# Second cross attention: turning the probabilities against a diagonal of inverse sums

## The chip, the cores and the metric

The kernel runs on one core of one Trainium2 chip. The metric is the device time of one launch in microseconds (us), and less is better. A core has five engines that run their own instruction streams and wait for each other by semaphores: TensorE (PE in the profile, with PEld for its weight loads), VectorE (DVE), ScalarE (ACT), GpSimd (POOL) and SyncE (SP). Each stream is executed in the order in which it was written, so an instruction that waits holds up all behind it on its engine.

## The reference, cut to what matters

Two decoder layers of width 128 over 4 batches of 512 tokens, with a context of 77 rows. The part around the change is the cross attention of the second layer: 8 heads of 64, 512 queries that come from the tokens, and 512 + 77 keys.

```python
xn = layernorm(x, gm, bm)                      # x here: the context, 77 rows
ln = layernorm(latents, gl, bl)                # latents: the 512 tokens
q = ln @ Wq
kv_input = jnp.concatenate([xn, ln], axis=-2)  # 589 keys
k, v = jnp.split(kv_input @ Wkv, 2, axis=-1)
q, k, v = (heads(q), heads(k), heads(v))
sim = jnp.einsum('bhid,bhjd->bhij', q / scale, k)
sim = sim - jnp.max(sim, axis=-1, keepdims=True)
attn = jax.nn.softmax(sim, axis=-1)
out = jnp.einsum('bhij,bhjd->bhid', attn, v)
return out @ Wout                              # heads joined again
```

## The kernel before

All data of a batch stay in SBUF, and each engine's program is written out by hand; batches follow each other in a loop of four. Every matrix product here is in fp32. The second cross attention works on 32 units per batch (`UNITS`). Unit i is one head and one tile of 128 queries; two units of a loop turn j, 2j and 2j + 1, are the two heads of a pair v = j // 4 for query tile t = j % 4. Three PSUM regions and three probability buffers `PBX` are used in turn by i % 3.

A unit goes round the engines like this:

- PE, `scores(j)` (L1355 and L1361): scores of both units against 512 token keys and 77 context keys. It waits until exp(2j - 2) has left its PSUM region and `move_context(2j - 2)` is done.
- DVE, `maximum(i)` (L2223): the negated row maximum over 589 columns.
- ACT, `exp(i)` (L1777): exponentials into `PBX`, with the row's sum added up into column i of `xsums` (the trace shows a second instruction that reads the accumulator).
- PE, `turn(k)` (L1367 and L1371): the context part (77 columns) and the four 128x128 blocks are transposed against the identity, into PSUM.
- ACT, `move_context(k)` (L1785) and DVE, `move(k)` (L2230): the turned parts go to SBUF, to `PTC` and `PTX`. `turn(k)` waits until `move(k - 1)` has emptied bank 6.
- PE, `value(v, c)` (L1386): values of pair v with chunk c of the turned probabilities, added up over the five chunks in bank 7; each pair's chunks are spread over the turns of the next pair.
- ACT, `copy_values(v)` (L1789): the values of pairs 0 to 2 go to `OT`.

PE's order in turn j is scores(j), turn(2j - 1), a projection of values in the first five turns, up to two value chunks, turn(2j). DVE's is maximum(2j), move(2j - 1), maximum(2j + 1), move(2j). ACT's is move_context(2j - 1), exp(2j), move_context(2j), exp(2j + 1), and then copies.

The probabilities are turned before they are divided by their sums; the division comes at the end, on the values. The inverse sums are made in two pieces (`invert_sums`, L2214). `spread_inverse(v)` (L1400) brings them to the layout of the values: 8 products of a broadcast column with the identity for each pair. DVE multiplies pairs 0 to 2 (`normalise`, L2219). The factors of the last pair are copied to `last_factors` by ACT (L1804) and multiplied in by DVE (L2247). PE then runs value(3, 0 to 4), `project_pairs(0, 3)` and `project_pairs(3, 1)` (L1407), and DVE adds the result to the residual (L2249).

Other lines that appear in the rows: L1494 is a product of the expert network with 128x128 operands; L1719 and L1723 are ACT copies from PSUM in other stages, the second with a bias of one value per partition; L1608 is an ACT operation on a 128x128 tile within SBUF.

Of the kernel before, what the change touches and what calls it, by code (L numbers as in the profile page):

```python
# [9 lines left out]
ALU = mybir.AluOpType  # L10
ACT = mybir.ActivationFunctionType
# [24 lines left out]
def decoder_kernel(nc, x, ctx_1024, qkv_w, qkv_b, qn_scale, qn_bias, kn_scale, kn_bias, ttt_gate, ttt_val,  # L36
# [4 lines left out]
    with stack:  # L41
# [3 lines left out]
        def sem(name):  # L45
            return stack.enter_context(nc.semaphore(name))
# [214 lines left out]
        def first_turn(n):  # L261
# [10 lines left out]
                             "probs_T_ready", "values_ready", "values_copied"))  # L272

        UNITS, XG = 4 * 8, 8
        s_xi, s_xsp, s_xn, s_xfac, s_cturned = (
            sem("x1_" + n) for n in ("sums_inverted", "spread", "values_normalised", "factors_moved", "context_turned"))

        (m_parts, m_picked, m_stacked, m_scores, m_max, m_split, m_turned, m_rows, m_scoresT, m_exp, m_acc01,
         m_acc, m_sums, m_inv, m_spread, m_norm, m_values, m_outs) = (sem("m_" + w) for w in (
# [409 lines left out]
        PTX = [PTA[:, 2048 * r:2048 * r + 2048].rearrange("p (k q) -> p k q", k=4) for r in range(3)]  # L689
        PTX.append(OTA[:, 2048:4096].rearrange("p (k q) -> p k q", k=4))  # L690
        PTC = KMA[:, 2560:4608].rearrange("p (h q) -> p h q", h=4)
        last_factors = QXA[:, 0:512]
        PT0 = [buf[0:CTX, at:at + 2048].rearrange("p (g q) -> p g q", g=4)
               for buf, at in ((PTA, 4096), (VA, 0), (VA, 2048), (OTA, 2048))]
        Y0 = KMA[:, 0:512].rearrange("p (t d) -> p t d", d=D)
# [255 lines left out]
        def _(pe):  # L951
# [320 lines left out]
            for b in range(BATCH):  # L1272
# [90 lines left out]
                    last.then_inc(s_scores, 1)  # L1363

                def turn(k):
                    pe.wait_ge(s_exp, b * UNITS + k + 1)
                    T.transpose(PSUM[0:CTX, 2 * (k % 3) + 1, P:2 * P], PBX[k % 3][:, SEQ:XK], ident[:, :]).then_inc(s_cturned, 1)  # L1367
                    if k:
                        pe.wait_ge(s_moved, b * UNITS + k)
                    for c in range(4):  # L1370
                        last = T.transpose(PSUM[:, 6, c * P:(c + 1) * P], PBX[k % 3][:, c * P:(c + 1) * P], ident[:, :])  # L1371
                    last.then_inc(s_turned, 1)

                def value(v, c):
                    if c == 0:
                        pe.wait_ge(s_moved, b * UNITS + XG * (v + 1))
                        pe.wait_ge(s_cmoved, b * UNITS + XG * (v + 1))
                        if v:
                            pe.wait_ge(s_outs, b * 3 + v)
                        else:  # L1380
                            pe.wait_ge(s_e_vs, b * 5 + 5)
                    rows = P if c < 4 else CTX
                    for e in range(2):
                        h = 2 * v + e
                        probs = PTX[h % 4][:, c, :] if c < 4 else PTC[0:CTX, h % 4, :]
                        last = T.matmul(PSUM[e * XD:(e + 1) * XD, 7, :], VX[0:rows, c, h * XD:(h + 1) * XD],  # L1386
                                        probs, start=(c == 0), stop=(c == 4))
                    if c == 4:
                        last.then_inc(s_values, 1)

                def spread_inverse(v):
                    k = (4, 5, 2, 0)[v]
                    pe.wait_ge(s_cmoved, b * UNITS + UNITS - 2)
                    if v >= 2:
                        pe.wait_ge(s_exp, b * UNITS + UNITS)
                    pe.wait_ge(s_xi, b * 2 + (2 if v == 3 else 1))
                    for t in range(QT):
                        for e in range(2):
                            i = XG * v + 2 * t + e
                            last = T.matmul(PSUM[e * XD:(e + 1) * XD, k, t * P:(t + 1) * P],  # L1400
                                            xsums[:, i:i + 1].to_broadcast([P, XD]), ident[:, :], start=True, stop=True)
                    last.then_inc(s_xsp, 1)

                def project_pairs(first, n):
                    for v in range(first, first + n):
# [5 lines left out]
                for j in range(UNITS // 2 + 1):  # L1411
# [9 lines left out]
                            value(pair, c)  # L1421
                    if j < UNITS // 2:
                        turn(2 * j)
                for v in range(4):
                    spread_inverse(v)
                for c in range(5):
                    value(3, c)
                pe.wait_ge(s_xfac, b + 1)
                pe.wait_ge(s_xn, b * 4 + 3)
                project_pairs(0, 3)  # L1430
                pe.wait_ge(s_xn, b * 4 + 4)
                project_pairs(3, 1)


# [139 lines left out]
        def _(act):  # L1574
# [169 lines left out]
            for b in range(BATCH):  # L1744
# [35 lines left out]
                def move_context(k):  # L1780
                    (v, t), e = divmod(k // 2, QT), k % 2
                    act.wait_ge(s_cturned, b * UNITS + k + 1)
                    if v >= 2 and t == 0 and e == 0:
                        act.wait_ge(s_values, b * 4 + v - 1)
                    A.activation(PTC[0:CTX, (2 * v + e) % 4, t * P:(t + 1) * P], PSUM[0:CTX, 2 * (k % 3) + 1, P:2 * P], ACT.Copy)                        .then_inc(s_cmoved, 1)  # L1785

                def copy_values(v):
                    act.wait_ge(s_values, b * 4 + v + 1)
                    A.activation(OT[:, v, :], bank(7), ACT.Copy).then_inc(s_outs, 1)  # L1789

                for j in range(UNITS // 2):
                    if j:
                        move_context(2 * j - 1)
                    exp(2 * j)
                    move_context(2 * j)
                    exp(2 * j + 1)
                    if j < 5:
                        copy_projected(j)
                    if j >= 8 and j % QT == 0:
                        copy_values(j // QT - 2)  # L1800
                move_context(UNITS - 1)
                copy_values(2)
                act.wait_ge(s_xsp, b * 4 + 4)
                A.activation(last_factors, bank(0), ACT.Copy).then_inc(s_xfac, 1)  # L1804


                rows_T()
# [60 lines left out]
        def _(dve):  # L1868
# [301 lines left out]
            for b in range(BATCH):  # L2170
# [36 lines left out]
                for p in range(4):  # L2207
                    dve.wait_ge(s_e_k, b * 4 + p + 1)
                    kb = 512 * (4 + 2 * (p % 2))
                    Vv.tensor_copy(KX[:, p, :], PSF[:, kb:kb + XK]).then_inc(s_e_ks, 1)  # L2210
                def invert_sums(first, n):
                    dve.wait_ge(s_exp, b * UNITS + XG * (first + n))
                    sums = xsums[:, XG * first:XG * (first + n)]
                    Vv.reciprocal(sums, sums).then_inc(s_xi, 1)  # L2214

                def normalise(v):
                    dve.wait_ge(s_xsp, b * 4 + v + 1)
                    dve.wait_ge(s_outs, b * 3 + v + 1)
                    Vv.tensor_tensor(OT[:, v, :], OT[:, v, :], bank((4, 5, 2)[v]), ALU.mult).then_inc(s_xn, 1)  # L2219

                def maximum(i):
                    at = 1024 * (i % 3)
# [9 lines left out]
                for j in range(UNITS // 2):  # L2232
                    dve.wait_ge(s_scores, b * (UNITS // 2) + j + 1)
                    maximum(2 * j)
                    if j:
                        move(2 * j - 1)
                    maximum(2 * j + 1)
                    if j == UNITS // 2 - 2:
                        invert_sums(0, 3)
                    move(2 * j)  # L2240
                move(UNITS - 1)
                invert_sums(3, 1)
                for v in range(3):
                    normalise(v)
                dve.wait_ge(s_xfac, b + 1)
                dve.wait_ge(s_values, b * 4 + 4)
                Vv.tensor_tensor(OT[:, 3, :], bank(7), last_factors, ALU.mult).then_inc(s_xn, 1)  # L2247
                dve.wait_ge(s_e_o, b + 1)
                Vv.tensor_tensor(xs, PSUM[:, 0:4, 0:D], xs, ALU.add)  # L2249

# [142 lines left out]
```

## Time and profile before

| what | us |
|---|---|
| median of 3 runs | 2002.82 |
| lowest and highest run | 2001.36, 2003.3 |
| the profiled execution, its own time | 2002.89 |
| its span in the trace | 2001.2 |
| TensorE, busy | 1747.9 (87%) |
| VectorE, busy | 1084.5 (54%) |
| ScalarE, busy | 845.2 (42%) |
| GpSimd, busy | 514.9 (26%) |
| mean granted TensorE clock | 0.935 of full |

The times above are of whole launches; the span runs from the first to the last instruction in the trace. Busy times are sums over stages of different kinds. The changed stage occurs four times, once per batch; the first one begins at 654.32 us of the span and its last instruction, the add of L2249, starts at 730.82.

### The profile page before, as it was taken

The page shows a single profiled execution, that of the slowest core. Times are in us where ns is not written, and L with a number is a line of the kernel's source. Part 1 is how long each engine was busy: PE and PEld are TensorE (multiplying, and loading weights), DVE is VectorE, ACT ScalarE, POOL GpSimd, SP SyncE. Part 2 cuts the span into 40 slices and gives each one's busy share as a digit, 9 for nine tenths or more (in the row PEclk, how much of TensorE's full clock was granted, in tenths as well). Part 3 has the DMA queues.
Part 4 walks back from the last instruction along what each step waited for, and adds up shares of the span by engine and source line. Part 5 has one row for each costly group of instructions (what it writes and reads, how often), then busy time and mean ns, then how long its engine had stood idle before and what let it go on. Part 6 is the DMA issues. An engine that isn't in the chain of part 4 may idle for free.

```text
span 2001.2 us, 27188 instructions
## 1 busy us (share of the span) xinstructions
PE 1747.9 (87%) x10505; PEld 996.0 (50%) x10505; DVE 1084.5 (54%) x2162; ACT 845.2 (42%) x1406; POOL 514.9 (26%) x574
## 2 busy tenths in 40 slices
PE   4599789896898988898989889998988998989888
PEld 3354645553434555573455546634555473455556
DVE  4577467464463656346646553563646346646542
ACT  2222222222463536345635444463536345635442
POOL 2377077230063003003700120063003002700120
PEclk7799899897889999898999899989999898999999
DMA  7000000000000000000000000000000000000000
GB/s 212 0 1 1 1 0 0 0 1 1 0 1 1 1 1 2 1 1 6 1 1 1 1 1 1 6 1 1 1 1 1 1 1 6 1 1 1 1 1 6
DMA packets 18260, 13.27 MB, mean 7 GB/s; under 512 B 7643, under 2 KB 14783, under 8 KB 18143
## 3 DMA queue, kind: packets, MB, share of 16 engines
q1 hardware_dynamic: 17951, 11.65, 2.1%
q8 instruction: 79, 1.29, 0.3%
q14 instruction: 38, 0.31, 0.1%
q10 hardware_dynamic: 192, 0.02, 0.0%
HBM read 10.55 MB, written 1.05 MB: 6 GB/s over the span
## 4 chain that ended last, share of the span: by engine, by line
PE 65%; issue 10%; DVE 7%; POOL 6%; ACT 6%; POOLq 5%; DVEq 1%; DMA 0%; SPq 0%
PE PSUM L1307 7%; PE PSUM L1484 6%; PE PSUM L1494 5%; PE PSUM L429 4%; PE PSUM L1386 4%; PE PSUM L1355 3%; PE PSUM L385 3%; PE PSUM L1371 2%; POOLq L873 2%; POOLq L871 2%; POOL OTA L875 2%; POOL OTA L870 2%; PE PSUM L1453 2%; PE PSUM L407 2%; PE PSUM L1367 2%
## 5 line engine op out<-in xcount | busy, mean ns | idle before, releaser
L585 DVE TENSOR_REDUCE negmax<-PSUM 128x2 f32<-128x1024 f32 (+3 forms) x256 | 256.3, 1015 | 117.5 <-PE PSUM L391 62.3
L234 POOL TENSOR_TENSOR rstd<-var,neg_half 128x4 f32<-128x4 f32 (+1 forms) x33 | 33.5, 1015 | 909.4 <-DVE var L224 824.0
L567 ACT ACTIVATE PTA<-PSUM 128x1024 f32<-128x1024 f32 (+1 forms) x224 | 214.0, 962 | 95.6 <-PE PSUM L429 94.9
L1494 PEld LDWEIGHTS PSUM<-W,PTA 128*128 128x128 f32 x1024 | 133.2, 192 | 57.8 <-issue 55.1
L1824 ACT ACTIVATE PTA<-PSUM,V 128x512 f32<-128x512 f32 x128 | 87.8, 686 | 162.2 <-PE PSUM L1484 162.1
L1307 PE MATMUL PSUM<-PTA,VA 128*64 128x512 f32 x512 | 146.0, 648 | 4.7 <-ACT OTA L546 2.2
L647 POOL TENSOR_TENSOR QXA<-QXA,PTA 128x1024 f32<-128x1024 f32 x56 | 132.8, 2372 | 35.1 <-ACT PTA L567 31.7
L1484 PE MATMUL PSUM<-YT,W 128*128 128x512 f32 x256 | 140.9, 640 | 0.0
L1494 PE MATMUL PSUM<-W,PTA 128*128 128x128 f32 x1024 | 134.5, 275 | 0.0
L429 PE MATMUL PSUM<-QSTACK,KSTACK 64*128 64x512 f32 (+3 forms) x512 | 111.0, 453 | 21.9 <-ACT PTA L567 8.5
L2223 DVE TENSOR_REDUCE nmax<-PSUM 128x1 f32<-128x589 f32 x128 | 97.6, 765 | 35.4 <-PE PSUM L1361 35.4
L385 PE MATMUL PSUM<-KSTACK,QSTACK 64*128 64x512 f32 (+3 forms) x512 | 103.0, 405 | 11.9 <-ACT QSTACK L535 4.5
L429 PEld LDWEIGHTS PSUM<-QSTACK,KSTACK 64*128 64x128 f32 x512 | 46.5, 188 | 104.5 <-ACT PTA L567 52.4
L643 POOL TENSOR_TENSOR QXA<-PTA 128x1024 f32<-128x1024 f32 x28 | 66.1, 2360 | 118.0 <-ACT PTA L567 118.0
L2230 DVE COPY PTA<-PSUM 128x512 f32<-128x512 f32 x96 | 66.3, 691 | 39.4 <-PE PSUM L1371 39.4
L2323 DVE SCALAR_TENSOR_TENSOR Y<-PSUM,comb,Y 128x128 f32<-128x128 f32 x112 | 31.5, 344 | 99.1 <-PE PSUM L1494 98.3
L541 ACT ACTIVATE QSTACK<-PSUM 32x512 fp32r<-32x512 f32 (+1 forms) x96 | 56.7, 590 | 59.0 <-PE PSUM L407 58.6
L1777 ACT ACTIVATE PB<-PSUM,nmax 128x589 f32<-128x589 f32 x88 | 65.6, 746 | 34.1 <-DVE nmax L2223 34.1
L1355 PE MATMUL PSUM<-KMA,QXA 64*128 64x512 f32 x256 | 72.3, 641 | 0.0
L656 POOL TENSOR_TENSOR tri_turn<-ones_col 128x1 f32<-128x1 f32 x128 | 24.7, 193 | 175.3 <-ACT PTA L567 175.2
L1785 ACT ACTIVATE KMA<-PSUM 77x128 f32<-77x128 f32 x128 | 34.9, 273 | 80.7 <-PE PSUM L1367 80.7
L385 PEld LDWEIGHTS PSUM<-KSTACK,QSTACK 64*128 64x128 f32 x512 | 51.0, 193 | 29.6 <-DVE negmax L585 10.4
(421 smaller groups left out, 3615.8 us busy)
## 6 DMA issues: line engine op xcount, KB each, us to landing
W<-in_L_ffn_W_dram SPq DMA_DIRECT2D x1, 2048.0 KB
out_dram<-X SPq DMA_DIRECT2D x4, 256.0 KB, 2.3
PTA<-in_L_attn_Wc_dram SPq DMA_DIRECT2D x1, 640.0 KB
PTA<-in_L_attn_Wo_dram SPq DMA_DIRECT2D x1, 512.0 KB
Wkv<-in_L_xattn_Wkv_dram SPq DMA_DIRECT2D x1, 512.0 KB
KMA<-in_L_attn_ttt_proj_dram SPq DMA_DIRECT2D x1, 256.0 KB
QXA<-in_L_ffn_w_up_dram SPq DMA_DIRECT2D x1, 256.0 KB
QXA<-in_L_ffn_w_down_dram SPq DMA_DIRECT2D x1, 256.0 KB
```

Source lines behind the costliest of these rows:

```text
L385: last = T.matmul(PSUM[:, k + e, at:at + w], QSTACK[rows, s, t * P:(t + 1) * P], KSTACK[rows, s, 0:w], start=True, stop=not a.causal)
L429: last = T.matmul(PSUM[:, a.scoresT_bank(k) + e, at:at + w], KSTACK[rows, s, c * P:(c + 1) * P], QSTACK[rows, s, a.first(c):SEQ], start=Tr ...
L567: A.activation(probs, PSUM[:, at:at + 2, 0:probs.shape[2]], ACT.Exp).then_inc(m_exp, 1)
L585: last = Vv.tensor_reduce(negmax[:, s % 2, t, :], PSUM[:, k:k + 2, at:at + a.width(t)], AX.X, ALU.max, negate=True)
L647: last = g.tensor_tensor(total, total, a.probsT(s, c), ALU.add)
L1307: last = T.matmul(PSUM[e * VD:(e + 1) * VD, 6, :], V1[:, c, h * VD:(h + 1) * VD], full.probsT(s, c)[:, e, :], start=(c == 0), stop=(c == Q ...
L1355: T.matmul(bank(2 * ((2 * j + e) % 3)), QX[rows, v, t * P:(t + 1) * P], KX[rows, v, 0:SEQ], start=True, stop=True)
L1386: last = T.matmul(PSUM[e * XD:(e + 1) * XD, 7, :], VX[0:rows, c, h * XD:(h + 1) * XD], probs, start=(c == 0), stop=(c == 4))
L1484: T.matmul(bank(m % 2), W1[:, e, m * P:(m + 1) * P], YT[:, :], start=True, stop=True).then_inc(s_f_h, 1)
L1494: last = T.matmul(PSUM[:, 2 + e % 2, t * P:(t + 1) * P], HE[:, e % 2, m, t * P:(t + 1) * P], W2[:, e, m, :], start=(m == 0), stop=(m == M ...
L1824: A.activation(HE[:, e % 2, m, :], bank(m % 2), ACT.Relu, bias=V[:, B1C + e * M + m:B1C + e * M + m + 1])\
L2223: Vv.tensor_reduce(nmax[:, 0, i % 3:i % 3 + 1], PSF[:, at:at + XK], AX.X, ALU.max, negate=True).then_inc(s_max, 1)
```

## The change

The probabilities of a unit are now divided by their sum while they are turned. DVE inverts the sum of each unit by itself (`invert_sum(i)`, one column). ACT makes a 128x128 matrix with these inverses on its diagonal (`diagonal(i)`: a copy of the identity with a per-partition scale) into one of three buffers `DIAG`. PE turns the five pieces of a unit by ordinary products with this matrix as the moving operand, where it had transposes against the identity. `turn(k)` waits for the diagonal, in place of the exponentials. The spreading of inverses, the normalisation of the values, the factors of the last pair and their semaphores leave the tail; the values of the last pair are copied as those of the others. On ACT, exp now stands ahead of move_context for both units.

```diff
-        s_xi, s_xsp, s_xn, s_xfac, s_cturned = (
-            sem("x1_" + n) for n in ("sums_inverted", "spread", "values_normalised", "factors_moved", "context_turned"))
+        s_xi, s_xd, s_cturned = (sem("x1_" + n) for n in ("sums_inverted", "diagonal_ready", "context_turned"))
...
-        last_factors = QXA[:, 0:512]
+        DIAG = [PTA[:, 6144 + P * r:6144 + P * (r + 1)] for r in range(3)]
...
                 def turn(k):
-                    pe.wait_ge(s_exp, b * UNITS + k + 1)
-                    T.transpose(PSUM[0:CTX, 2 * (k % 3) + 1, P:2 * P], PBX[k % 3][:, SEQ:XK], ident[:, :]).then_inc(s_cturned, 1)
+                    pe.wait_ge(s_xd, b * UNITS + k + 1)
+                    T.matmul(PSUM[0:CTX, 2 * (k % 3) + 1, P:2 * P], PBX[k % 3][:, SEQ:XK], DIAG[k % 3],
+                             start=True, stop=True).then_inc(s_cturned, 1)
                     if k:
                         pe.wait_ge(s_moved, b * UNITS + k)
                     for c in range(4):
-                        last = T.transpose(PSUM[:, 6, c * P:(c + 1) * P], PBX[k % 3][:, c * P:(c + 1) * P], ident[:, :])
+                        last = T.matmul(PSUM[:, 6, c * P:(c + 1) * P], PBX[k % 3][:, c * P:(c + 1) * P], DIAG[k % 3],
+                                        start=True, stop=True)
                     last.then_inc(s_turned, 1)
...
-                def spread_inverse(v):
...
-                for v in range(4):
-                    spread_inverse(v)
                 for c in range(5):
                     value(3, c)
-                pe.wait_ge(s_xfac, b + 1)
-                pe.wait_ge(s_xn, b * 4 + 3)
                 project_pairs(0, 3)
-                pe.wait_ge(s_xn, b * 4 + 4)
+                pe.wait_ge(s_outs, b * 4 + 4)
                 project_pairs(3, 1)
...
+                def diagonal(i):
+                    act.wait_ge(s_xi, b * UNITS + i + 1)
+                    if i >= 3:
+                        act.wait_ge(s_turned, b * UNITS + i - 2)
+                    A.activation(DIAG[i % 3], ident[:, :], ACT.Copy, scale=xsums[:, i:i + 1]).then_inc(s_xd, 1)
+
                 for j in range(UNITS // 2):
                     if j:
+                        diagonal(2 * j - 1)
+                    exp(2 * j)
+                    if j:
                         move_context(2 * j - 1)
-                    exp(2 * j)
+                    diagonal(2 * j)
+                    exp(2 * j + 1)
                     move_context(2 * j)
-                    exp(2 * j + 1)
...
+                diagonal(UNITS - 1)
+                copy_values(2)
                 move_context(UNITS - 1)
-                copy_values(2)
-                act.wait_ge(s_xsp, b * 4 + 4)
-                A.activation(last_factors, bank(0), ACT.Copy).then_inc(s_xfac, 1)
+                copy_values(3)
...
+                def invert_sum(i):
+                    dve.wait_ge(s_exp, b * UNITS + i + 1)
+                    Vv.reciprocal(xsums[:, i:i + 1], xsums[:, i:i + 1]).then_inc(s_xi, 1)
...
                     maximum(2 * j)
                     if j:
+                        invert_sum(2 * j - 1)
                         move(2 * j - 1)
                     maximum(2 * j + 1)
-                    if j == UNITS // 2 - 2:
-                        invert_sums(0, 3)
+                    invert_sum(2 * j)
                     move(2 * j)
+                invert_sum(UNITS - 1)
                 move(UNITS - 1)
-                invert_sums(3, 1)
-                for v in range(3):
-                    normalise(v)
-                dve.wait_ge(s_xfac, b + 1)
-                dve.wait_ge(s_values, b * 4 + 4)
-                Vv.tensor_tensor(OT[:, 3, :], bank(7), last_factors, ALU.mult).then_inc(s_xn, 1)
```

## Rows read from the trace of the kernel before

**Rows 1.** The page: busy time, share of the span and instructions of each engine.

```profile
PE 1747.9 (87%) x10505; PEld 996.0 (50%) x10505; DVE 1084.5 (54%) x2162; ACT 845.2 (42%) x1406; POOL 514.9 (26%) x574
```

**Rows 2.** Windows: us, busy of each engine, granted clock, DMA share, GB/s.

```profile
654.30:718.60 64.30, 61.90 (x357) 32.66 (x358) 44.70 (x66) 37.25 (x103) 0.00 (x0) 1.00 0.00 1
718.60:731.00 12.40, 12.19 (x120) 8.59 (x116) 3.39 (x7) 1.19 (x2) 0.00 (x0) 1.00 0.01 1
755.00:760.00 5.00, 3.06 (x27) 1.96 (x28) 2.90 (x6) 2.88 (x4) 1.11 (x4) 1.00 0.01 2
```

**Rows 3.** Timeline, one cycle: start us, length us, engine, line, what, xcount, idle before.

```profile
697.16 1.13 PE L1355 MATMUL PSUM<-KMA,QXA 64*128 64x512 f32 x4
698.40 0.33 PE L1367 MATMUL PSUM<-ident,PB 128*77 128x128 f32 x1
698.52 0.77 DVE L2223 TENSOR_REDUCE nmax<-PSUM 128x1 f32<-128x589 f32 x1 [0.56 <-PE PSUM L1361]
698.57 0.60 PE L1371 MATMUL PSUM<-ident,PB 128*128 128x128 f32 x4
699.21 0.69 DVE L2230 COPY PTA<-PSUM 128x512 f32<-128x512 f32 x1
699.32 0.75 ACT L1777 ACTIVATE PB<-PSUM,nmax 128x589 f32<-128x589 f32 x1 [0.28 <-DVE nmax L2223]
699.82 0.76 DVE L2223 TENSOR_REDUCE nmax<-PSUM 128x1 f32<-128x589 f32 x1
699.97 0.19 ACT L1777 ACTIVATION_READ_ACCUMULATOR PB<-PSUM,nmax 128x1 f32 x1
700.22 0.33 PE L1367 MATMUL PSUM<-ident,PB 128*77 128x128 f32 x1
700.92 1.13 PE L1355 MATMUL PSUM<-KMA,QXA 64*128 64x512 f32 x4
701.02 0.69 DVE L2230 COPY PTA<-PSUM 128x512 f32<-128x512 f32 x1 [0.45 <-PE PSUM L1371]
```

**Rows 4.** Timeline: first, second and last scores of the stage, and its tail.

```profile
654.32 1.13 PE L1355 MATMUL PSUM<-KMA,QXA 64*128 64x512 f32 x4
658.08 1.13 PE L1355 MATMUL PSUM<-KMA,QXA 64*128 64x512 f32 x4
712.95 1.13 PE L1355 MATMUL PSUM<-KMA,QXA 64*128 64x512 f32 x4
717.44 0.33 PE L1367 MATMUL PSUM<-ident,PB 128*77 128x128 f32 x1 [0.66 <-ACT PB L1777]
719.06 3.67 PE L1400 MATMUL PSUM<-ident,rsums 128*64 128x128 f32 x64
719.27 0.60 ACT L1789 ACTIVATE OTA<-PSUM 128x512 f32<-128x512 f32 x1 [1.19 <-PE PSUM L1386]
722.55 0.59 PE L1386 MATMUL PSUM<-PTA,VA 128*64 128x512 f32 x1
726.95 3.84 PE L1407 MATMUL PSUM<-Wout,OTA 128*128 128x128 f32 x32
730.82 0.69 DVE L2249 TENSOR_TENSOR X<-PSUM,X 128x512 f32<-128x512 f32 x1 [3.00 <-PE PSUM L1407]
```

**Rows 5.** One line's instructions: xcount, duration ns min/median/max, first and last start us.

```profile
L1608 ACT ACTIVATE KMA<-KMA x4: 309/309/309, 43.0 to 79.8; 128x128 f32<-128x128 f32 x4
L2214 DVE RECIPROCAL rsums<-rsums x8: 193/242/292, 711.8 to 1845.0; 128x24 f32<-128x24 f32 x4, 128x8 f32<-128x8 f32 x4
```

**Rows 6.** Groups by line: xcount, busy us, mean ns, idle before and its releaser.

```profile
L1719 ACT ACTIVATE YT<-PSUM 128x512 f32<-128x512 f32 x4 | 2.4, 597 | 13.6 <-PE PSUM L1132 13.6
L1723 ACT ACTIVATE QXA<-PSUM,V 128x512 f32<-128x512 f32 x4 | 2.7, 687 | 5.8 <-PE PSUM L1233 5.8
L1785 ACT ACTIVATE KMA<-PSUM 77x128 f32<-77x128 f32 x128 | 34.9, 273 | 80.7 <-PE PSUM L1367 80.7
L1494 PE MATMUL PSUM<-W,PTA 128*128 128x128 f32 x1024 | 134.5, 275 | 0.0
```

More of the change, by code:

```diff
@@ L1378, in value @@
                         if v:
-                            pe.wait_ge(s_outs, b * 3 + v)
+                            pe.wait_ge(s_outs, b * 4 + v)
                         else:
@@ L1389, in value @@
                         last.then_inc(s_values, 1)
-                def spread_inverse(v):
[L1392 to L1402, printed above, removed]
                 def project_pairs(first, n):
@@ L2210, in _ @@
                     Vv.tensor_copy(KX[:, p, :], PSF[:, kb:kb + XK]).then_inc(s_e_ks, 1)
[L2211 to L2219, printed above, removed]
+                def invert_sum(i):
+                    dve.wait_ge(s_exp, b * UNITS + i + 1)
+                    Vv.reciprocal(xsums[:, i:i + 1], xsums[:, i:i + 1]).then_inc(s_xi, 1)
                 def maximum(i):
```

## Prediction

> **What bounds the kernel now.** I read the page's busy shares first: TensorE (PE) 87%, VectorE (DVE) 54%, ScalarE (ACT) 42% [rows 1]. These average over many stages, so next come windows over the changed stage, the second cross attention. Its loop fills 654.3 to 718.6 us, its tail lasts to about 731, and it occurs once per batch, four times in all. In the loop PE is busy 61.90 of 64.30 us, DVE 44.70, ACT 37.25, POOL not at all, and the clock is at 1.00 (the 2.4 GHz level) [rows 2]. PE looks like the bound, but its records overlap, so the timeline of one cycle j (two units, 2j and 2j+1) decides.
>
> Read there what ends each start [rows 3]. scores(j) starts at 697.16; DVE's first maximum starts at 698.52, 1.36 later; exp(2j) follows its end by 0.03 (699.32) and takes 0.75 + 0.19 us; turn(2j) starts at 700.22; scores(j+1) at 700.92. That makes 3.76 us: a chain over PE, DVE and ACT, closed because scores(j+1) stands behind turn(2j) in PE's order. DVE's move and second maximum (699.21, 699.82) lie beside it. In cycles with two value chunks PE's own work ends later. From the second scores to the last one 14 cycles pass in 712.95 - 658.08 = 54.87 us: 3.92 us each [rows 4]. The reader should keep both facts: the cycle is a chain of handovers, and one more link in it is paid about 15 times per batch.
>
> **Prices of the new parts.**
>
> Diagonal on ACT, 128x128 from SBUF with a per-partition scale: a 128x128 ACT copy within SBUF takes 0.309 us [rows 5]. A 128x512 activation takes 0.597 without and 0.687 with one per-partition operand, 0.090 more [rows 6]. I take 0.40. Bounds: 0.28 (a 77x128 PSUM copy is 0.273 [rows 6]) and 0.49 (twice the 0.090).
>
> Reciprocal of one column: the longest of the rows' reciprocals is 24 columns at 0.292, the shortest 8 columns at 0.193 [rows 5]: 0.0062 per column, so 0.15 for one. Bounds: 0 and 0.193.
>
> Products in place of transposes: the four transposes of a unit are four records in 0.60 us, the last lasting 0.27, so 0.11 apart [rows 3]. An fp32 product leaves two records (L1400: 64 for the 32 products of the four spread_inverse calls; L1407: 32 for 16 products), and L1407's 32 take 3.84 us, (3.84 - 0.27)/31 = 0.115 apart, with a new 128x128 weight each time [rows 4]. So one unit's five turned pieces become ten passes: five more at 0.11 = 0.55 us. Bounds: 0.107 and 0.131 each, the latter L1494's 134.5 us over 1024 [rows 6], 0.54 to 0.66. A turn held PE for 0.70 us (700.22 to 700.92) and let DVE's move start 0.80 after its own start (701.02) [rows 3]; after the change 1.25 and 1.35.
>
> The Trainium skill bears on this price: TensorE: Matmul & The Clock Gate, section Terms, calls the transpose mode four times faster for FP32. The rows show two passes of one transpose's length, a factor of two. By the page's factor a turn would have 20 passes' worth instead of ten; that is a rival below.
>
> Handovers: DVE to ACT 0.03 [rows 3], taken as 0.04; the exp's end (699.97 + 0.19 = 700.16) to PE 0.06 [rows 3], taken as 0.05.
>
> **The chain after the change.** What matters is not that DVE and ACT have room but where the new instructions stand in their orders. DVE does maximum(2j), invert(2j-1), move(2j-1), maximum(2j+1), invert(2j), move(2j). invert(2j-1) stands behind maximum(2j), so the inverse of a sum known since the previous cycle is made only after scores(j). turn(2j-1) now waits for it through ACT's diagonal; move(2j-1) waits for that turn; maximum(2j+1) and invert(2j) are queued behind the move; diagonal(2j), turn(2j) and scores(j+1) wait for invert(2j). Both turns of a cycle are in series. Event by event, us from scores(j):
>
> - 1.36 maximum(2j) starts [rows 3]; the next DVE instruction starts 0.69 later (698.52 to 699.21): invert(2j-1) 2.05 to 2.20
> - +0.04: diagonal(2j-1) 2.24 to 2.64; +0.05: turn(2j-1) 2.69, PE free at 3.94
> - 2.69 + 1.35: move(2j-1) 4.04; the next starts 0.61 later (699.21 to 699.82 [rows 3]): maximum(2j+1) 4.65
> - +0.69: invert(2j) 5.34 to 5.49; +0.04: diagonal(2j) 5.53 to 5.93
> - +0.05: turn(2j) 5.98; +1.25: scores(j+1) 7.23
>
> Hidden beside it: exp(2j) runs behind diagonal(2j-1), 2.64 to 3.58, before invert(2j) wants it at 5.34. One value chunk costs 4.40/5 = 0.88 (722.55 to 726.95 [rows 4]); two after 3.94 end at 5.70, before 5.98, so the long cycles cost no more than the short ones. exp(2j+1) is queued behind diagonal(2j), 5.93 to 6.87, and move_context(2j) ends at 7.14, while the next context scores come about 0.9 after 7.23. If the chain were shorter, these would surface: PE's own sum is the old 3.92 plus 1.1.
>
> Cycle: 7.23 against 3.92 = +3.31, for 14 cycles +46.3 us.
>
> First cycle: 3.76 before (654.32 to 658.08 [rows 4]); no odd unit yet, so only one inverse, diagonal and turn enter: 0.04 + 0.15 + 0.04 + 0.40 + 0.55 = +1.18.
>
> End, from the last scores: before, 712.95 to 730.82 = 17.87 (DVE's add, L2249) [rows 4]. After: turn(30) at 5.98, move(30) 7.33, invert(31) 7.94 to 8.09, diagonal(31) 8.13 to 8.53, turn(31) 8.58 to 9.83. value(2,4) to copy_values(2): 719.27 - (717.44 + 0.70) = 1.13 [rows 3, 4], so 10.96, copy 0.60, then the moved-back move_context(31) 0.27 (to 11.83). value(3,0), which waits for it, 11.88. Then 4.40 to the projection and 3.87 from there to the add, as before (722.55 to 726.95 to 730.82 [rows 4]): 20.15. copy_values(3) hides behind the projection of pairs 0 to 2 (24 passes of 0.115 = 2.8). The 32 spread products and the factor multiplications leave, but they stood ahead of a value(3) that began at 722.55 - 712.95 = 9.60 and now begins at 11.88. End: +2.28.
>
> Per batch 1.18 + 46.3 + 2.28 = 49.8, times four = +199. The profiled execution took 2002.89 us around its 2001.2 span; the median of the runs is 2002.82. Forecast 2202 us.
>
> The clock: the chain leaves PE gaps of 1.4 us (1.25 to 2.69) and at most 1.2 more, 5.1 to 6.0 busy of 7.23. A stretch with PE busy 3.06 of 5 us stands at clock 1.00 [rows 2], so I leave it there.
>
> **Own range.** Per cycle two inverses, two diagonals, two sets of five passes: low 2 x (-0.15 - 0.12 - 0.01) = -0.56, high 2 x (0.04 + 0.09 + 0.11) = +0.48; times 60 (15 cycles, four batches) -34 to +29. Five handovers misread by 0.04 each add 12 either way: 2156 to 2243.
>
> **Rivals.**
>
> A. DVE's order doesn't bind, since something lets the move and second maximum go early. Then the chain is 1.36 + 0.80 + 0.94 + 0.04 + 0.15 + 0.04 + 0.40 + 0.05 + 1.25 = 5.03, +1.11 per cycle: 4 x (15.5 + 1.18 + 2.28) = +76, 2079 us. For it: DVE is busy only 44.70 of 64.30. Against: its instructions start in order in every row. 6%.
>
> B. The gaps drop the clock to 1.2 GHz. Scores (1.25) and both turns (1.1 each) double, +3.4 per cycle: +205 more, 2407 us. Against: the 3.06-of-5 stretch. 3%.
>
> C. A product costs four transposes: 10 passes more in each of two turns, +2.2 per cycle, +132: 2334 us. For it stands only the page named above; against it L1407. 2%.
>
> D. Faster: passes, inverse and diagonal all vanish in waiting, and only the tail's spreads count. value(3,0) would wait for copy_values(2) alone (719.87) instead of 722.55, -2.6 per batch [rows 4]: 1992 us. It decides only if a cycle grows by less than 2.6/15 = 0.17 us, and five passes alone exceed that in a chain that closes through the turn. 1%.
>
> Forecast 85%; 3% lies between A and no change (1% of it within 0.2%). My range, 2155 to 2245, is the forecast's own, and holds some 80% with what I may have missed in it. 0.2% is about what a measurement tells from no change: faster 1%, same 1%, slower 98%.
>
> **What the profile would show.** Each scores pair of L1355 7.2 us after the last (A: 5.0); DVE reciprocals 128x1, 128 of them, each right behind a maximum; ACT 128x128 activations of 0.40; moves of L2230 waiting over 1 us for PE; L1371's line with 1024 records; clock 1.00. Wrong would be: a maximum(2j+1) starting before turn(2j-1) is moved, a granted clock of 0.5, or products spaced over 0.2.

## The result, and the profile after

The changed kernel takes 2222.17 us (median of 4 runs, 2221.09 to 2223.46) against 2003.03 us for the kernel before in the same comparison. The ratio is 1.109, with a 95% interval from 1.1078 to 1.1105: slower by 219 us, where 199 were forecast (2202, range 2155 to 2245).

The page after, its first part; it answers to [rows 1]:

```profile
PE 1832.4 (82%) x10889; PEld 1073.2 (48%) x10889; DVE 1086.6 (49%) x2266; ACT 876.0 (39%) x1534; POOL 515.1 (23%) x574
```

PE has 84.5 us more work, DVE 2.1 and ACT 30.8, and the span grew by 220.5. All shares fell: the engines do a little more and wait much more. Windows over the loop and the tail of the first changed stage, against [rows 2] (us, busy of each engine, granted clock, DMA share, GB/s):

```profile
654.40:768.90 114.50, 79.57 (x506) 50.73 (x504) 47.49 (x95) 44.23 (x133) 0.00 (x0) 1.00 0.00 1
768.90:781.20 12.30, 10.63 (x66) 6.60 (x66) 0.94 (x4) 1.75 (x4) 0.00 (x0) 1.00 0.01 2
```

The loop takes 114.5 us where it took 64.3; PE was busy 96% of it and is now 69%, at a granted clock of 1.00 still. The timeline of one cycle, against [rows 3]:

```profile
695.68 1.13 PE L1354 MATMUL PSUM<-KMA,QXA 64*128 64x512 f32 x4
...
697.04 0.77 DVE L2210 TENSOR_REDUCE nmax<-PSUM 128x1 f32<-128x589 f32 x1 [0.56 <-PE PSUM L1360]
697.73 0.15 DVE L2206 RECIPROCAL rsums<-rsums 128x1 f32<-128x1 f32 x1
697.92 0.40 ACT L1779 ACTIVATE PTA<-ident,rsums 128x128 f32<-128x128 f32 x1 [2.66 <-DVE rsums L2206]
...
698.65 1.06 PE L1371 MATMUL PSUM<-PTA,VA 128*128 128x128 f32 x8
...
699.74 0.69 DVE L2217 COPY OTA<-PSUM 128x512 f32<-128x512 f32 x1 [1.86 <-PE PSUM L1371]
...
700.35 0.76 DVE L2210 TENSOR_REDUCE nmax<-PSUM 128x1 f32<-128x589 f32 x1
...
701.03 0.15 DVE L2206 RECIPROCAL rsums<-rsums 128x1 f32<-128x1 f32 x1
701.22 0.40 ACT L1779 ACTIVATE PTA<-ident,rsums 128x128 f32<-128x128 f32 x1 [2.01 <-DVE rsums L2206]
...
702.94 1.13 PE L1354 MATMUL PSUM<-KMA,QXA 64*128 64x512 f32 x4
```

Read it down the engine column: PE, DVE, ACT, PE, DVE, ACT, PE. Scores to scores is 7.26 us. The bracket on a diagonal (2.66, 2.01) is ACT's idle time before it, ended by a reciprocal; the one on the move (1.86) is DVE's, ended by the turn. The chain of waits over the same window says the same in order of time (start, length, what; a piece ends where the next begins):

```profile
697.04 0.77 DVE nmax L2210
697.81 0.08 DVE rsums L2206
697.89 0.02 issue
697.92 0.41 ACT PTA L1779
698.33 0.04 issue
698.37 0.44 PE PSUM L1366 x2
698.81 0.91 PE PSUM L1371 x8
699.72 0.02 issue
699.74 0.69 DVE OTA L2217
700.43 0.68 DVE nmax L2210
701.11 0.08 DVE rsums L2206
701.19 0.02 issue
701.22 0.41 ACT PTA L1779
701.63 0.04 issue
701.67 0.44 PE PSUM L1366 x2
```

There is no slack: both maxima, both inverses, both diagonals, the move and both turns stand one behind the other. (The 0.08 of the inverse is what is left of it when the maximum's record has ended.) A turn takes 1.27 us of the chain, from 701.67 to the next scores at 702.94.

The prices, from the groups by line (xcount, busy us, mean ns, idle before and its releaser):

```profile
L1779 ACT ACTIVATE PTA<-ident,rsums 128x128 f32<-128x128 f32 x128 | 51.4, 401 | 273.1 <-DVE rsums L2206 273.1
...
L1371 PE MATMUL PSUM<-PTA,PB 128*128 128x128 f32 x704 | 93.0, 275 | 0.0
```

The diagonal takes 0.401 us (forecast 0.40), the reciprocal 0.153 (0.15). ACT stood idle for 273 us ahead of its diagonals. L1371 has 704 + 320 = 1024 records, two per product.

The stage from its first scores to its last add took 76.5 us in each batch [rows 4]; now it takes 126.7 in each, +50.2 (forecast +49.8). Four times 50.2 is 201. The rest of the excess is not in this stage. From the add to the first reciprocal of the next stage, the causal attention, whose code is unchanged, the four batches took 66.59, 68.24, 66.86 and 66.44 us before and take 71.62, 71.90, 71.91 and 71.68 now: +19.0 together. 201 + 19 = 220.

Windows over that next stage in batch 0, each kernel's taken from its own add; the column before the last two is the granted clock. From 0 to 12 and from 12 to 24 us behind the add it is 0.72 and 1.00 in both kernels: the first fall is common to them. The rows are the stretches from 24 to 28 and from 28 to 42 us behind it. The kernel before:

```profile
754.82:758.82 4.00, 2.06 (x19) 1.19 (x17) 2.05 (x5) 2.65 (x3) 0.53 (x2) 1.00 0.00 0
758.82:772.82 14.00, 12.59 (x145) 7.59 (x139) 10.32 (x18) 8.83 (x13) 6.01 (x24) 1.00 0.01 2
```

and the changed kernel:

```profile
805.17:809.17 4.00, 2.06 (x16) 1.25 (x14) 2.05 (x5) 2.42 (x4) 0.28 (x2) 0.94 0.00 0
809.17:823.17 14.00, 13.60 (x90) 8.18 (x92) 7.15 (x12) 6.02 (x8) 4.28 (x17) 0.53 0.00 1
```

The same thin stretch, 2.06 us busy of 4, is followed by full clock in the one and by 0.53, nearly all of it the 1.2 GHz level, in the other: 90 matmul records where there were 145 in 14 us. This is called the second fall below.

### The profile page after: what moved, and what is told of

Its sections match the earlier page's. It is cut to its first block, busy times and chain, and to the rows that moved or that the text cites. A ratio compares the mean times of both kernels' runs of the same rounds, so it can differ in the third digit from the quotient of the medians.

```text
span 2221.7 us, 28268 instructions
## 1 busy us (share of the span) xinstructions
PE 1832.4 (82%) x10889; PEld 1073.2 (48%) x10889; DVE 1086.6 (49%) x2266; ACT 876.0 (39%) x1534; POOL 515.1 (23%) x574
## 4 chain that ended last, share of the span: by engine, by line
PE 61%; DVE 12%; issue 9%; ACT 7%; POOL 5%; POOLq 4%; DVEq 1%; DMA 0%; SPq 0%
PE PSUM L1306 6%; PE PSUM L1468 5%; PE PSUM L1371 5%; PE PSUM L1478 5%; DVE nmax L2210 4%; PE PSUM L428 4%; PE PSUM L1354 3%; PE PSUM L384 3%; PE PSUM L1366 3%; ACT PTA L1779 2%; POOLq L872 2%; POOLq L870 2%; POOL OTA L874 2%; POOL OTA L869 2%; PE PSUM L1437 2%
## 5 line engine op out<-in xcount | busy, mean ns | idle before, releaser
L1779 ACT ACTIVATE PTA<-ident,rsums 128x128 f32<-128x128 f32 x128 | 51.4, 401 | 273.1 <-DVE rsums L2206 273.1
L2217 DVE COPY PTA<-PSUM 128x512 f32<-128x512 f32 x96 | 66.4, 691 | 178.9 <-PE PSUM L1371 178.9
L428 PE MATMUL PSUM<-QSTACK,KSTACK 64*128 64x512 f32 (+3 forms) x512 | 116.1, 474 | 22.2 <-ACT PTA L566 9.0
L1366 PE MATMUL PSUM<-PTA,PB 128*77 128x128 f32 x176 | 39.0, 303 | 98.1 <-ACT PTA L1779 97.3
L384 PE MATMUL PSUM<-KSTACK,QSTACK 64*128 64x512 f32 (+3 forms) x512 | 108.5, 425 | 11.7 <-ACT QSTACK L534 4.7
L1371 PE MATMUL PSUM<-PTA,PB 128*128 128x128 f32 x704 | 93.0, 275 | 0.0
L1366 PEld LDWEIGHTS PSUM<-PTA,PB 128*77 128x77 f32 x176 | 18.7, 145 | 142.9 <-ACT PTA L1779 142.9
L1371 PEld LDWEIGHTS PSUM<-PTA,PB 128*128 128x128 f32 x704 | 85.5, 192 | 0.0
```

Of the source, the lines that this page charges most:

```text
L384: last = T.matmul(PSUM[:, k + e, at:at + w], QSTACK[rows, s, t * P:(t + 1) * P], KSTACK[rows, s, 0:w], start=True, stop=not a.causal)
L428: last = T.matmul(PSUM[:, a.scoresT_bank(k) + e, at:at + w], KSTACK[rows, s, c * P:(c + 1) * P], QSTACK[rows, s, a.first(c):SEQ], start=Tr ...
L1366: T.matmul(PSUM[0:CTX, 2 * (k % 3) + 1, P:2 * P], PBX[k % 3][:, SEQ:XK], DIAG[k % 3], start=True, stop=True).then_inc(s_cturned, 1)
L1371: last = T.matmul(PSUM[:, 6, c * P:(c + 1) * P], PBX[k % 3][:, c * P:(c + 1) * P], DIAG[k % 3], start=True, stop=True)
L1779: A.activation(DIAG[i % 3], ident[:, :], ACT.Copy, scale=xsums[:, i:i + 1]).then_inc(s_xd, 1)
```

## The experiments

Unless said otherwise the kernels are the changed one with the edit shown. "Stage" is first scores to last add of one batch, undisturbed by what follows.

**e1: the first inverse ahead of the scores.**

```diff
                 for j in range(UNITS // 2):
+                    if j:
+                        invert_sum(2 * j - 1)
                     dve.wait_ge(s_scores, b * (UNITS // 2) + j + 1)
                     maximum(2 * j)
                     if j:
-                        invert_sum(2 * j - 1)
                         move(2 * j - 1)
```

> The changed kernel with one line moved: on DVE the inverse of unit 2j-1 is made before the wait for scores(j), not behind maximum(2j). Theory of the serial chain (both turns of a cycle in series behind DVE's order): turn(2j-1) then starts about 1.35 after scores(j) and not 2.7, the second half of the chain keeps its length (move, second maximum, inverse, diagonal, turn), so the cycle falls from 7.25 to about 5.9 us; 15 cycles in four batches give -82, some 2140 us. Rival (the price is that of the added instructions on their engines, wherever they stand): no change, 2222 us. Apart from this the clock of the following unchanged stage may give or take up to 5 us per batch.

Measured: 2124.07 us, ratio 1.059 (1.0564 to 1.0625). Cycles of 5.93 us, stage 106.8 (-20.0 per batch). Timeline:

```profile
693.99 1.13 PE L1354 MATMUL PSUM<-KMA,QXA 64*128 64x512 f32 x4
694.10 0.69 DVE L2217 COPY PTA<-PSUM 128x512 f32<-128x512 f32 x1 [1.86 <-PE PSUM L1371]
694.71 0.15 DVE L2206 RECIPROCAL rsums<-rsums 128x1 f32<-128x1 f32 x1
694.89 0.40 ACT L1779 ACTIVATE PTA<-ident,rsums 128x128 f32<-128x128 f32 x1 [1.33 <-DVE rsums L2206]
...
695.35 0.44 PE L1366 MATMUL PSUM<-PTA,PB 128*77 128x128 f32 x2
```

The turn now follows scores by 1.36 us and not by 2.69: inverse and diagonal are made while PE computes the scores. One instruction in another place of one queue took 79.8 us off four stages. The spans differ by 98.6 (2221.7 and 2123.1). The next stage accounts for the rest: its four stretches are back at 66.5 to 66.7 us, 20.7 less in sum, and some 2 us are lost elsewhere. The theory holds, its rival falls.

**e2: both inverses early.** DVE's order becomes inverse 2j-1, wait for scores, maximum 2j, maximum 2j+1, inverse 2j, move 2j-1, move 2j.

```diff
                     maximum(2 * j)
-                    if j:
-                        move(2 * j - 1)
                     maximum(2 * j + 1)
                     invert_sum(2 * j)
+                    if j:
+                        move(2 * j - 1)
                     move(2 * j)
```

(The diff is against e1.)

> The changed kernel with DVE's order in a cycle: inverse 2j-1, then scores, maximum 2j, maximum 2j+1, inverse 2j, move 2j-1, move 2j. Theory of the serial chain: nothing of turn(2j) waits for move(2j-1) and the second maximum any more; diagonal 2j starts right behind exp(2j), and the cycle falls to about 5.05 us in turns with one value chunk (chain over exp, inverse, diagonal and turn) and 5.6 in turns with two (PE's own work), 5.2 on average; about 2098 us. This is the rival A of the prediction made real (2079 there). Rival: the added instructions cost their own time, no change from e1.

Measured: 2089.62 us, ratio 1.041 (1.0382 to 1.0446). Cycles of 4.95 and, with two value chunks, 5.76; stage 94.6 (-12.1 more). Timeline:

```profile
692.77 0.75 ACT L1761 ACTIVATE VA<-PSUM,nmax 128x589 f32<-128x589 f32 x1 [0.86 <-DVE nmax L2210]
...
693.65 0.16 DVE L2206 RECIPROCAL rsums<-rsums 128x1 f32<-128x1 f32 x1 [0.23 <-ACT VA L1761]
...
693.85 0.40 ACT L1779 ACTIVATE PTA<-ident,rsums 128x128 f32<-128x128 f32 x1
...
694.30 0.45 PE L1366 MATMUL PSUM<-PTA,VA 128*77 128x128 f32 x2
```

The inverse of the even unit now waits for the exponentials, its true producer, and the turn follows at 0.65. PE is busy 78.81 of the 81.38 us from 655.12 to 736.50, so little waiting is left. The time lies 8 us under the 2098 expected. This is the smallest price of the diagonal that a change of order gave, and it still loses to the kernel before.

**e3: transposes behind the diagonal.** The wait, the inverses and the diagonals stay; the turning is done against the identity. The division by the sums is left out of the output.

```diff
-                    T.matmul(PSUM[0:CTX, 2 * (k % 3) + 1, P:2 * P], PBX[k % 3][:, SEQ:XK], DIAG[k % 3],
-                             start=True, stop=True).then_inc(s_cturned, 1)
+                    T.transpose(PSUM[0:CTX, 2 * (k % 3) + 1, P:2 * P], PBX[k % 3][:, SEQ:XK], ident[:, :]).then_inc(s_cturned, 1)
...
-                        last = T.matmul(PSUM[:, 6, c * P:(c + 1) * P], PBX[k % 3][:, c * P:(c + 1) * P], DIAG[k % 3],
-                                        start=True, stop=True)
+                        last = T.transpose(PSUM[:, 6, c * P:(c + 1) * P], PBX[k % 3][:, c * P:(c + 1) * P], ident[:, :])
```

> The changed kernel, but the five pieces of a unit are turned by transposes against the identity, while inverse, diagonal and the wait for it stay; the output leaves out the division by the sums. Theory: the two turns of a cycle each lose 5 passes of 0.11 us from the chain, 7.25 to 6.15; with the first and the last cycle 17.6 per batch, -70: 2152 us. Rival (products cost as much as transposes in waiting, the whole price is the new wait): 2222. Rival C of the prediction (factor four) would give -130 and more.

Measured: 2177.19 us, ratio 1.086 (1.0828 to 1.0888). The cycle is 6.12 us where the clock is full, as expected, but the saving is 45 us and not 70: the four stages take 118.5, 117.1, 118.6 and 117.1 us, 35.5 less than in the changed kernel, and the stage behind them gives 9.2 more, because two of its four stretches are back at the old length (66.71 and 66.49; the others 72.36). Windows inside the first changed stage:

```profile
655.00:675.00 20.00, 12.33 (x71) 6.86 (x70) 9.86 (x19) 9.75 (x28) 0.00 (x0) 1.00 0.00 1
700.00:710.00 10.00, 6.71 (x33) 3.40 (x31) 4.87 (x10) 4.36 (x13) 0.00 (x0) 0.85 0.00 0
710.00:720.00 10.00, 7.24 (x30) 3.56 (x26) 3.81 (x8) 2.98 (x10) 0.00 (x0) 0.64 0.00 0
```

Here the clock falls within the stage, and two cycles of the first batch take 8.28 and 8.32 us. That is rival B of the prediction, seen in a neighbour of the changed kernel. The changed kernel itself has the same waits with ten passes per turn in place of five; in the same 20 us PE is busy 13.71 in it against 12.33 here, and its loop stayed at 1.00 throughout. The Trainium skill, TensorE: Matmul & The Clock Gate, Part 4: PE-mode transpose, says that transposes do not count as engine activity in the way that matmuls do. These two kernels agree with that, but they also differ in busy time, so they do not prove it.

**e4: products without the diagonal.** Turned by products against the identity, behind the exponentials; no inverses, no diagonals (their lines on DVE and ACT, taken out too, are not shown); the division by the sums is left out of the output.

```diff
-                    pe.wait_ge(s_xd, b * UNITS + k + 1)
-                    T.matmul(PSUM[0:CTX, 2 * (k % 3) + 1, P:2 * P], PBX[k % 3][:, SEQ:XK], DIAG[k % 3],
+                    pe.wait_ge(s_exp, b * UNITS + k + 1)
+                    T.matmul(PSUM[0:CTX, 2 * (k % 3) + 1, P:2 * P], PBX[k % 3][:, SEQ:XK], ident[:, :],
...
-                        last = T.matmul(PSUM[:, 6, c * P:(c + 1) * P], PBX[k % 3][:, c * P:(c + 1) * P], DIAG[k % 3],
+                        last = T.matmul(PSUM[:, 6, c * P:(c + 1) * P], PBX[k % 3][:, c * P:(c + 1) * P], ident[:, :],
```

> The changed kernel, turned by products against the identity, with the wait for the exponentials as before the change; no inverses and no diagonals, so the output leaves out the division by the sums; the tail is that of the changed kernel. Theory: without the new link PE's own sum decides, 1.25 + 1.25 + 0.88 + 1.25 = 4.63 us in turns with one value chunk and 5.5 with two, 4.85 on average against 3.92 before the change; tail 1.7 shorter than before the change; 2051 us, with up to 5 us per batch either way from the clock of the next stage. If the chain through the diagonal were cheap, this would lie near the changed kernel's 2222.

Measured: 2061.29 us, ratio 1.028 (1.0245 to 1.0316). Stage 89.7 us. PE's timeline of one cycle:

```profile
696.42 1.13 PE L1354 MATMUL PSUM<-KMA,QXA 64*128 64x512 f32 x4
...
697.94 1.06 PE L1371 MATMUL PSUM<-ident,VA 128*128 128x128 f32 x8
...
700.21 1.06 PE L1371 MATMUL PSUM<-ident,PB 128*128 128x128 f32 x8
701.20 1.13 PE L1354 MATMUL PSUM<-KMA,QXA 64*128 64x512 f32 x4
```

4.78 us, of which PE has no idle time to speak of (with two chunks 5.64): here PE's own work is the bound, 0.15 above the sum expected. The passes alone make the kernel slower: four stages of 89.7 in place of 76.5 are 53 us. The profiled execution (2064.21) lies 13 above the 2051 expected. Of this 7.4 are in neither of the two stages: behind the causal attention of batch 0 the clock falls in a stretch where it was full before. The windows 80 to 120 us behind the reciprocal, first of the kernel before, then of e4:

```profile
877.41:917.41 40.00, 37.30 (x193) 25.02 (x191) 22.55 (x62) 16.47 (x22) 2.01 (x2) 1.00 0.00 1
...
890.55:930.55 40.00, 37.56 (x173) 25.06 (x172) 17.77 (x54) 12.43 (x18) 2.01 (x2) 0.80 0.00 1
```

**e5: the tail alone.** e4 with transposes: the loop of the kernel before (but for ACT's order, which is that of the changed kernel; the cycles are 3.76 and 4.51 us as before), without the spread products, the normalisation and the factors, and so without the division by the sums.

> The changed kernel's tail with the loop of the kernel before: transposes against the identity behind the exponentials, no inverses, no diagonals, no spread products and no factors; the output leaves out the division by the sums. It measures what the removal is worth by itself. Theory: cycles of 3.76 and 4.51 as before the change, value(3,0) some 2.6 us earlier per batch: -10, 1992 us, with up to 5 us per batch either way from the clock of the next stage. Rival: the tail's products were hidden and their removal gives nothing, 2003.

Measured: 2018.93 us, ratio 1.0087 (1.007 to 1.0104): slower than the kernel before with less work, against both expectations, and beyond the 5 us per batch that the first allowed for the clock. In batch 0 the stage takes 74.13 us, 2.37 less than before, as expected. In the other three it takes 75.8, because the clock falls in the tail; windows of the tail, up to the add, in batch 0 and in batch 1:

```profile
713.00:727.50 14.50, 13.04 (x81) 7.47 (x77) 3.44 (x5) 3.35 (x9) 0.00 (x0) 1.00 0.00 0
...
1094.00:1107.60 13.60, 12.17 (x64) 6.39 (x62) 1.38 (x2) 2.26 (x6) 0.00 (x0) 0.87 0.00 0
```

And the causal attention behind it takes 72.30, 71.69, 71.62 and 71.42 us, 19 more than before in sum. The loop ahead of it has the old density, so thin work in the changed loop is not needed for that loss. Nor is it enough for it: e1's loop is thinner than the old one (PE busy 74.61 of 88.00 us from 654 to 742, 85% against 96%), and none of its four stretches has the loss; e2's loop is as dense as the old one, and all four have it. The tail is not the cause by itself either: e1 and e4 leave out the spread products as e5 does, and their stretches take 66.5 to 66.7 us (one of e4's 68.67).

**e6, e7, e8: a shift ahead of the stage.** An extra DVE operation on a scratch tile, once, in batch 0, ahead of the second cross attention; e6 has one, e7 two, both in the changed kernel; e8 has two in the kernel before.

```diff
                 Vv.tensor_tensor(xs, xs, Y2[:, :, :], ALU.add)
+                for _ in range(2 if b == 0 else 0):
+                    dve.drain()
+                    Vv.scalar_tensor_tensor(Y2[:, :, :], Y2[:, :, :], SLOPE, Y2[:, :, :], ALU.mult, ALU.max)
```

> The changed kernel with one extra DVE operation of about 0.7 us (on a scratch tile) once, in batch 0 ahead of the second cross attention, so that all that follows is shifted by some 0.8 us. In the changed kernel the stage after the changed one is 5 us longer in each batch at a half granted clock. Theory (whether the clock falls there depends on the moment at which its thin stretch begins, and the change only moved that moment): the loss vanishes in some or all of the four batches, and the kernel becomes faster by up to 20 us although it has more work. Rival (the thinner TensorE work of the changed stage lowers the clock of the next one): the loss stays in all four, +0.8 us.

> As the run before it with two extra operations, a shift of some 1.5 us. Same theories: by the moment the loss comes and goes with the shift, between -19 and +1.5 us; by the thinner work it stays, +1.5 us.

> The kernel before the change with the same two extra operations in batch 0, a shift of some 1.5 us. By the moment: the next stage loses some 5 us in several batches here too, without anything of the change, up to 2003 + 1.5 + 20 = 2024 us. By the thinner work: 2004.5 us.

Measured: 2227.67 us (1.1107 to 1.1141 of before), 2226.95 (1.1097 to 1.1131) and 2010.63 (1.0027 to 1.0058). In e6 and e7 the loss stayed in all four batches (71.7 to 72.3), as the rival had it and not the theory of the moment. The stage began 2.8 us later in both, in place of 0.8 and 1.5, so the two runs tried one shift and not two. The launches lie 5 us above the changed kernel's 2222.17, more than either theory added. In e8 batch 0 of the kernel before takes 71.58 us in the causal attention where it took 66.59, and the other three 67.04, 67.02 and 66.46. That is one batch, where the theory had several, and all four launches of e8 took 2010.6 us or more. So the loss can be had without the change. Even no edit at all can bring some such loss: one of seven launches of the kernel before, from the comparison for e1 to e4, took 2012.35 us at a granted clock of 0.932, the other six 2000.9 to 2004.51.

**e9 to e12: a shift behind the stage.** The same operation behind the add that ends the stage, in batch 0: once in the changed kernel (e9), once and three times in the kernel before (e10, e11), once in e5 (e12).

```diff
                 Vv.tensor_tensor(xs, PSUM[:, 0:4, 0:D], xs, ALU.add)
+                for _ in range(1 if b == 0 else 0):
+                    dve.drain()
+                    Vv.scalar_tensor_tensor(Y2[:, :, :], Y2[:, :, :], SLOPE, Y2[:, :, :], ALU.mult, ALU.max)
```

> The changed kernel with one extra DVE operation (0.77 us) in batch 0, right behind the add that ends the changed stage. In the changed kernel the granted clock falls 3.6 us after that add, returns some 10.5 us after it and falls again in a thin stretch about 27 us after it; in the kernel before it fell 2.5 us after the add, returned at 9.3 and did not fall again. Theory (the moment decides): in batch 0 the second fall goes and the stretch from the add to the first reciprocal of the next stage takes 66.6 + 0.8 us and not 71.6. Rival (thinner work in the changed stage is the cause): 71.6 + 0.8. The later batches move with it and may go either way.

> The kernel before the change with the same operation at the same place, the control: by both theories batch 0 has no second fall, 66.6 + 0.8 us from the add to the reciprocal.

> The kernel before the change with three such operations there (2.3 us). By the moment: the second fall appears in batch 0, 66.6 + 2.3 + about 5 = 74 us, with nothing of the change in the kernel. By the thinner work of the changed stage: 68.9 us.

> The run with only the tail removed (2018.93 us; second falls in all four batches, after a loop of the old density) with the same operation in batch 0. By the moment: batch 0 loses its second fall, 72.3 + 0.8 - 5 = 68 us, and the later batches can go either way; the time lies between 1992 + 1 and 2019 + 1 us. The output leaves out the division by the sums.

Measured, whole launches: 2219.27 us (1.1062 to 1.1099), 2010.59 (1.0026 to 1.0054), 2009.02 (1.002 to 1.0045) and 2017.59 (1.0061 to 1.0095). What tells them apart is batch 0, add to reciprocal: 67.47, 71.93, 74.00 and 72.76 us. The windows 28 to 42 us behind the add, first of e9, then of e11:

```profile
810.45:824.45 14.00, 12.57 (x141) 7.70 (x141) 10.26 (x18) 8.82 (x13) 6.14 (x24) 1.00 0.01 2
```

```profile
757.63:771.63 14.00, 12.42 (x82) 8.10 (x82) 7.32 (x12) 6.67 (x9) 4.32 (x16) 0.57 0.00 0
```

e9 lost the second fall in batch 0 (and kept it in the other three, 71.65 to 71.91 us), with nothing but 0.8 us of extra work in the program; e11 gained it in the kernel before. Both came as the theory of the moment had them. e10 and e12 did not: e10, the control, has a second fall too, and e12 kept its own.

The moment was not what I had worked from in three of the four. Where the extra operation stands behind the add, the add itself should not move; but in the profiled executions e9's came at 782.45 and not 781.17, e10's at 729.51 and e11's at 729.63 and not 730.82. These 1.2 to 1.3 us arose ahead of the edit, by nothing that I had changed, and are more than the 0.8 that e9 and e10 tried. In e12 the add stood where it had in e5 (727.63 against 727.55), so it is the cleanest trial of the 0.8 us, and there the fall stayed. So the four batches of e9 to e12 don't show that the shift is what switched the fall. What the runs do show is that neither the thin loop nor the changed tail decides it by itself; that the moment does is a conjecture.

## Why the prediction was right, step by step

**The queue order as the mechanism: right.** Forecast 7.23 us per cycle, measured 7.26, in short and long cycles alike; first cycle 4.94 forecast, 4.95 measured; last scores to the add 20.15 against 20.18. e1 and e2 take the two links out one after the other, and the cycle falls to 5.93 and to 4.95 or 5.76.

**The prices: right.** 0.401 and 0.153 us, two passes per product, turns of 1.27 where 1.25 was forecast. The price by the page's factor of four (rival C) is out: L1371's records per product are two.

**What each part costs**, by stage lengths of one batch at full clock:

| step | stage, us | difference |
|---|---|---|
| kernel before | 76.5 | |
| tail's products out (e5, batch 0) | 74.1 | -2.4 |
| products for transposes (e4) | 89.7 | +15.5 |
| inverse and diagonal, both early (e2) | 94.6 | +5.0 |
| inverse 2j behind the move and the maximum (e1) | 106.8 | +12.1 |
| inverse 2j-1 behind maximum 2j (changed kernel) | 126.7 | +20.0 |

The sum is +50.2. Taken in this order, the new link itself costs 5.0 and its place in DVE's order 32.1; another order of steps would share them out otherwise, since e2 also has the move behind the second maximum, which e4 has not. The removal that stands against it is worth 2.4, close to the 2.6 of rival D.

**Rival A** (DVE's order doesn't bind) was wrong for this kernel and is nearly what e2 made true: 2089.6 against its 2079. Its four stages grew by 72.5 us (4 x 18.1), where rival A had 76; the rest is the next stage's clock, 72.39, 71.05, 70.89 and 70.67 us from add to reciprocal, 16.9 more than before in sum.

**Rival B** (the clock) was placed in the wrong stage. In the changed stage the clock held, as forecast. But the sum ended with the stage: "The profiled execution took 2002.89 us ... Forecast 2202 us" carries everything outside at its old length, and that was the term that was off, by 19 of the 20 us that are missing. The unchanged causal attention ran most of the 14 us shown above at the lower clock. e8, e10 and e11 show that the kernel before can have the same loss without the change, and e9 that the changed kernel can be without it in a batch. Why the fall comes in one case and not in another stays open; e6, e7, e10 and e12 show that I could not set it at will. A granted clock near 0.5, which the prediction had named as a sign of being wrong, did appear, one stage behind the place where it was looked for.

The argument by which the prediction dismissed the clock was weak as well. By its own gaps, 1.4 and at most 1.2 us, PE is busy 4.6 to 5.5 of 7.23 us, and not 5.1 to 6.0; measured is 5.05 of 7.26 on average (79.57 of 114.50 us). That is still more than the 3.06 of 5 that it leaned on, but e3 lost the full clock in stretches where PE was busy for 6.71 and 7.24 of 10 us. One stretch at full clock did not show what another would do.

That the time fell into the range in spite of the 19 us was partly luck: its upper end stood 43 us above the forecast for prices and handovers, which all came out close, and it held no term for the clock of another stage.

## What to carry to other kernels

An instruction added to an in-order queue can cost what stands ahead of it and not its own length: write down where its operand is ready and what the queue is doing then. Here a 0.15 us reciprocal in the wrong slot cost 20 us per batch, and moving it was free. Moving normalisation from a short tail into every turn of a loop is a poor trade where the loop closes over that very step: 2.4 us were saved, and even the best order paid 18 more than before.

Steps of 5 us in a stage whose code is unchanged call for a look at the granted clock by windows before they are explained by the edit.

## What the runs showed of the hardware that I had not expected

- With one and the same program text for a stage, the time from add to reciprocal was 66.4 to 67.0 us in some batches and 70.7 to 72.4 in others, with three between 68.2 and 68.7 (all profiled executions, without the batches that had an extra operation in the stretch).
- Without any edit ahead of it, the first changed stage began between 653.0 and 655.7 us in the profiled executions of eleven kernels. A shift of 0.8 us is less than that.
- The kernel with less TensorE work was the slower one: e5 has 128 fewer products than the kernel before and took 0.9% longer, at a granted clock of 0.922 against 0.935.
- e3, with transposes, kept the full clock while PE was busy for 12.33 of 20 us and lost it 25 us further on, at 6.71 and 7.24 of 10; the changed kernel, with products in their place, was busy for 13.71 of 20 and kept it to the end of the stage.
